# Three more split down products whose low parts VectorE makes from a bank, and four gate/up banks in place of five

## What is computed

```python
B, S, D = (2, 256, 256); I = 128; E = 32; K = 4
logits = flat @ router_w.T
scores = jnp.sqrt(jax.nn.softplus(logits))
_, idx = jax.lax.top_k(scores + expert_bias, K)
...
def _clamped_swiglu(x, wg, wu, wd):
    g = jnp.clip(x @ wg.T, -ALPHA, ALPHA)
    u = jnp.clip(x @ wu.T, -ALPHA, ALPHA)
    return jax.nn.silu(g) * u @ wd.T

def body(acc, xs):
    wg, wu, wd, p = xs
    return (acc + p[:, None] * _clamped_swiglu(flat, wg, wu, wd), None)
out, _ = jax.lax.scan(body, jnp.zeros_like(flat), (gate_w, up_w, down_w, probs.T))
out = out + _clamped_swiglu(flat, shared_gate_w, shared_up_w, shared_down_w)
x = x + out
```

## Time and profile before

| | |
|---|---|
| median of three runs | 72.20 us (72.13, 72.20, 73.02) |
| the profiled execution | 72.16 us, of which the span 70.3 us |
| granted clock of TensorE | 0.997 of full speed |
| TensorE, busy | 65.7 us (93%) |
| POOL, busy | 54.0 us (77%) |
| VectorE, ScalarE, busy | 46.9 us (67%), 46.0 us (65%) |
| read from HBM | 15.52 MB |

### The profile page before, as it was taken

The page is one execution under the profiler, slowest core; times in us unless marked ns, Lnnn a source line. Parts: engine busy times, 40 slices in busy tenths (PEclk is TensorE's granted clock), DMA queues, the critical chain, the costliest instruction groups (busy, mean ns, idle before and its releaser), DMA issues.

```text
span 70.3 us, 1581 instructions
## 1 busy us (share of the span) xinstructions
PE 65.7 (93%) x544; PEld 49.2 (70%) x546; DVE 46.9 (67%) x132; ACT 46.0 (65%) x101; POOL 54.0 (77%) x59
## 2 busy tenths in 40 slices
PE   5999998998998999999999999999999999999940
PEld 2347565787864486648787878888887888788830
DVE  0058489584779536599999907758995887697440
ACT  0604547669988665678989399999968852275220
POOL 6430005499999994999799999999999999999000
PEclk9999999999999999999999999999999999999998
DMA  0899999999999999999999997100000000000002
GB/s 0 261 282 304 343 424 390 235 332 422 429 410 408 389 403 400 403 374 347 384 415 394 396 389 274 54 6 0 0 9 0 0 0 0 0 0 0 5 0 75
DMA packets 6343, 15.75 MB, mean 224 GB/s; under 512 B 704, under 2 KB 1472, under 8 KB 6336
## 3 DMA queue, kind: packets, MB, share of 16 engines
q1 hardware_dynamic: 6048, 15.39, 59.7%
q10 hardware_dynamic: 288, 0.27, 1.1%
HBM read 15.52 MB, written 0.13 MB: 223 GB/s over the span
## 4 chain that ended last, share of the span: by engine, by line
PE 82%; DVE 7%; ACT 4%; POOL 3%; issue 1%
PE bP L581 22%; PE bY L614 7%; PE bY L603 6%; PE bE L444 6%; PE bE L581 6%; PE bXT L593 5%; PE bP L567 5%; PE bP L381 4%; PE bY L616 3%; PE bP L408 2%; DVE shifted L851 2%; POOL gu_w L347 2%; DVE row_max L849 2%; PE bXT L437 1%; ACT probs L669 1%
## 5 line engine op out<-in xcount | busy, mean ns | idle before, releaser
L347 POOL TENSOR_TENSOR gu_w<-gu_raw,gu_w 128x512 fp32r<-128x512 f32 x28 | 35.1, 1287 | 1.4 <-ACT gu_w L699 1.4
L581 PE MATMUL bP<-gu_w,xnT_parts 128*128 128x512 f32 x66 | 18.7, 418 | 0.0
L581 PEld LDWEIGHTS bP<-gu_w,xnT_parts 128*128 128x128 f32 x66 | 12.2, 189 | 3.0 <-issue 0.5
L1009 DVE SCALAR_TENSOR_TENSOR h<-gu_clip,gate,bP 128x128 f32<-128x128 f32 x26 | 7.8, 344 | 5.3 <-ACT bP L784 5.3
L955 DVE TENSOR_SCALAR gu_clip<-bP,clip_at 128x512 f32<-128x512 f32 x13 | 10.4, 806 | 1.1 <-PE bP L581 1.1
L692 ACT ACTIVATE gu_w<-gu_raw 128x1024 fp32r<-128x1024 f32 x9 | 9.4, 1048 | 1.1 <-issue 1.1
L353 POOL TENSOR_TENSOR gu_w<-dn_w,gu_w 128x512 fp32r<-128x512 f32 x8 | 10.0, 1309 | 0.0
L790 ACT ACTIVATE hT_parts<-bXT 128x256 fp32r<-128x256 f32 x11 | 4.2, 384 | 6.4 <-PE bXT L593 6.4
L784 ACT ACTIVATE bP<-gu_clip,rstd 128x256 f32<-128x256 f32 x13 | 6.2, 473 | 0.2 <-DVE gu_clip L955 0.2
L593 PE MATMUL bXT<-consts_sb,h 128*128 128x128 f32 x33 | 6.2, 271 | 0.0
L337 POOL TENSOR_TENSOR aw_sb<-aw_sb,lora_v 128x256 f32<-128x256 f32 x2 | 1.4, 727 | 6.1 <-DMA aw_sb<-attn_w_dram 6.1
(11 more groups left out here) (162 smaller groups left out, 124.3 us busy)
## 6 DMA issues: line engine op xcount, KB each, us to landing
gu_raw<-moe_w_dram SPq DMA_DIRECT2D x16, 512.0 KB, 9.7
dn_w<-moe_w_dram SPq DMA_DIRECT2D x16, 256.0 KB, 9.7
aw_sb<-attn_w_dram SPq DMA_DIRECT2D x2, 512.0 KB, 7.0
shared_sb<-shared_w_dram SPq DMA_DIRECT2D x1, 384.0 KB, 14.5
small_sb<-small_dram SPq DMA_DIRECT2D x1, 370.0 KB, 6.9
xwq_sb<-x_wq_dram SPq DMA_DIRECT2D x1, 256.0 KB, 3.5
lora_sb<-lora_dram SPq DMA_DIRECT2D x1, 256.0 KB, 4.3
ctx_sb<-ctx_kv_dram ACTq DMA_DIRECT2D x1, 192.0 KB, 3.1
```

The lines of the kernel that those rows point to most:

```text
L347: nc.gpsimd.tensor_tensor(gu_w[:, gu_slot(p), 1, cols], gu_raw[:, raw_slot(p), cols], gu_w[:, gu_slot(p), 0, cols], ALU.subtract).then_inc ...
L581: last = nc.tensor.matmul(bGU[n % 5][:, 0:GU], xnT_parts[:, a, k, :], gu_w[:, gu_slot(n - 1), w, k * GU:(k + 1) * GU], start=(k == 0 and a ...
L1009: last = nc.vector.scalar_tensor_tensor(h[:, n % 4, e], gu_clip[:, n % 4, e, 1, :], weight_e, bank[:, e * 2 * I:e * 2 * I + I], ALU.mult, ...
```

## The change

`LAST` goes from 11 to 14, so `FIRST` is 2 and units 3 to 16 have split down products. The low parts of the first three (units 3, 4, 5) are made by VectorE instead of POOL. VectorE does not read the raw weights: ScalarE first copies them into a bank (`dn_stage`), and VectorE subtracts the high part from the bank. The bank is bE, the fifth of the gate/up banks, which unit 4 is the last to use; units 6 to 16 go round over four banks, so that from unit 9 on `gate_up(n)` waits for `gate_h(n - 4)`, not `gate_h(n - 5)`. POOL makes eleven low parts as before, now those of units 6 to 16, and starts them behind pair 14 instead of 12. In ScalarE's loop `hT_unit(n)` and the new copies stand ahead of `gu_high(10 + n)`, not behind it.

```diff
-LAST = 11
-BETWEEN = 12
+LAST = 14
+STAGED = 3
+BETWEEN = 14
 FIRST = PAIRS - LAST
...
-        bGU = (bP[0][:, 0], bP[0][:, 1], bP[1][:, 0], bP[1][:, 1], bE)
+        bStage = bE
+
+        def bGU(n):
+
+            if n < 6:
+                return (bP[0][:, 0], bP[0][:, 1], bP[1][:, 0], bP[1][:, 1], bE)[n % 5]
+            return (bP[0][:, 1], bP[1][:, 0], bP[1][:, 1], bP[0][:, 0])[(n - 6) % 4]
...
                 if p >= BETWEEN:
-                    dn_low(p - BETWEEN)
-            for i in range(PAIRS - BETWEEN, LAST):
+                    dn_low(STAGED + p - BETWEEN)
+            for i in range(STAGED + PAIRS - BETWEEN, LAST):
                 dn_low(i)
...
             def gate_up(n):
 
                 if n > 5:
-                    pe.wait_ge(h_ready, n - 4)
+                    pe.wait_ge(h_ready, n - 4 if n < 9 else n - 3)
...
                     i = n - 1 - FIRST
-                    pe.wait_ge(dn_lo_ready, i + 1)
+                    if i < STAGED:
+                        pe.wait_ge(dn_lo_dve_ready, i + 1)
+                    else:
+                        pe.wait_ge(dn_lo_ready, i - STAGED + 1)
                     pe.wait_ge(hT_low_ready, i + 1)
...
+            def dn_stage(i):
+
+                if i:
+                    act.wait_ge(dn_lo_dve_ready, i)
+                else:
+                    act.wait_ge(h_ready, 5)
+                at = (FIRST + i) * 2 * D
+                nc.scalar.activation(bStage[:], dn_w[:, at:at + 2 * D], ACT.Copy).then_inc(stage_ready, 1)
+
...
             for n in range(1, PAIRS + 1):
                 if n + 2 <= PAIRS:
                     silu_unit(n + 2)
+                if 0 <= n - 2 < STAGED:
+                    dn_high(n - 2)
+                    dn_stage(n - 2)
+                hT_unit(n)
                 if EARLY + n < PAIRS:
                     gu_high(EARLY + n)
-                hT_unit(n)
-                if 0 <= n - 2 < UNITS:
-                    dn_high(n - 2)
...
+            def dn_low(i):
+
+                dve.wait_ge(stage_ready, i + 1)
+                dve.wait_ge(dn_hi_ready, i + 1)
+                nc.vector.tensor_tensor(dn_parts(i)[:, 1], bStage[:], dn_parts(i)[:, 0], ALU.subtract
+                                        ).then_inc(dn_lo_dve_ready, 1)
+
             for n in range(2, PAIRS + 1):
                 gate_h(n)
                 if n + 2 <= PAIRS:
                     clip(n + 2)
+                if 0 <= n - 4 < STAGED:
+                    dn_low(n - 4)
                 if n - 2 > FIRST:
                     hT_low(n - 2)
```

More of the change, by code:

```diff
@@ L254, in build @@
         dn_lo_ready = sem("dn_lo_ready")
+        dn_lo_dve_ready = sem("dn_lo_dve_ready")
+        stage_ready = sem("stage_ready")
         gu_hi_ready = sem("gu_hi_ready")
@@ L565, in gate_up_whole @@
             def gate_up_whole(n, k):
-                return nc.tensor.matmul(bGU[n % 5][:, 0:GU], xfT[:, k, :], gu_raw[:, raw_slot(n - 1), k * GU:(k + 1) * GU],
+                return nc.tensor.matmul(bGU(n)[:, 0:GU], xfT[:, k, :], gu_raw[:, raw_slot(n - 1), k * GU:(k + 1) * GU],
                                         start=(k == 0), stop=(k == DC - 1))
@@ L580, in gate_up @@
                         for a, w in HI_LO:
-                            last = nc.tensor.matmul(bGU[n % 5][:, 0:GU], xnT_parts[:, a, k, :],
+                            last = nc.tensor.matmul(bGU(n)[:, 0:GU], xnT_parts[:, a, k, :],
                                                     gu_w[:, gu_slot(n - 1), w, k * GU:(k + 1) * GU],
@@ L781, in silu_unit @@
                 width = 2 if n else 1
-                bank = bGU[n % 5] if n else bShared
+                bank = bGU(n) if n else bShared
                 dst = bank[:, 0:width * 2 * I].rearrange("p (e w i) -> p e w i", e=width, w=2)[:, :, 0, :]
```

## The result

The changed kernel took 75.06 us at the median of five executions (74.95 to 77.26), the kernel before 72.20 us; the ratio is 1.039, 95% interval 1.035 to 1.044. It is slower, by 2.9 us where 0.3 were forecast, and outside the forecast range (71.7 to 73.1).

What follows compares the result with a forecast made beforehand. TensorE alone was taken to bound the experts' part. The 0.46 us gain is taken and 0.8 given back at the wait before down(7): 72.16 + 0.34 = 72.5 us, range 71.7 to 73.1.

Steps and rivals of the forecast that it cites:

- the start of the sum: The kernel before's profiled time of 72.16 us, taken as the base to which the later start of down(7) was added.
- part 2: POOL's low part for down(7): without slips over at 54.00, asked for by TensorE at 54.27, slack 0.27 us.
- Part 1: Down(3), (4) and (5) become split, each shortening TensorE's path by 0.155 us: 0.46 us in all.
- Parts 3 and 4: ScalarE's queue falls 1.1 us behind by pair 13; POOL, waiting for its high parts, slips 0.93 us in sum.
- the last term of the sum: Start of down(7) moves from 54.73 to 55.00, +0.27 us, plus 0.07 for the weight load waiting with it.
- Part 5: VectorE's added subtracts and hT_low, and four banks: TensorE waits 0.05 and 0.07 us, inside the wait before down(7).
- The gain in full: Rival: ScalarE catches up, POOL slips under 0.3 us, nobody waits: 71.7 us, up to 72.2; 25%.
- VectorE slows POOL: Rival: POOL stands during VectorE's three subtracts, 0.69 us each, giving 73.9 us; 4%.
- A dear copy into the bank: Rival: `dn_stage` or the wait before it costs over 0.61 us start to start; 0.7 gives 73.0; 11%.

Runs made afterwards that it cites:

- the extra copy: Changed kernel with one more 128x512 ScalarE copy behind the first copy into the bank: 73.21 to 75.39 us, experts' part 40.92 against 40.42.
- The profile with direct subtracts: Changed kernel without the copies into the bank, VectorE subtracting from the raw weights in SBUF: 73.20 to 77.29 us, experts' part 40.90.

## Why the prediction was wrong

**The step that failed: the start of the sum.** It missed by 2.6 us (75.06 for 72.5), of which 1.9 are a term that its sum didn't have. The sum starts from 72.16, the one profiled execution, and takes the stretch before the first gate/up product as it was: a term put at nothing, without a reason. In the changed kernel TensorE's pace rose late, at 9.59 us in place of 5.10, and the first gate/up product started at 28.72 us in place of 26.84. The profile shows it for one of the five recorded executions; the times of the other four, 75.0 to 77.3, say the same. The range was built from the experts' part alone, though the kernel before has executions 2 us above its median as well; the three times that were shown (72.13 to 73.02) held none. The Trainium skill ("TensorE: Matmul & The Clock Gate", What's actually happening) says that the moment of the rise varies from run to run and puts its cost under 1% of a span; here the late rise cost 1.88 of 72.8 us, 2.6%.

How much of that was bad luck? That all five were late was a draw, but not a rare one: of the other twelve executions of the same kernel seven were late, and the median of all seventeen is 74.98. Where the rise was early, the changed kernel took 72.56, 73.08 and 73.30 us when it was run again, and 73.16 at the third time. For a forecast of 72.5 that is inside the range or up to 0.2 above it, and 1.1% above the kernel before. What misses even then is the 0.2 of part 2 and the 0.35 outside the span.

**Part 1** (0.155 us for a product). Right, as far as it can be read: two of them gave 0.2 to 0.4 where nobody was late, for a forecast of 0.31. What the step called "all the change can give" wasn't to be had with three.

**Parts 3 and 4** (the queue of ScalarE, the slip of POOL). Right to 0.05 us at each of the points above, and the extra copy confirms the chain nearly one for one (0.50 for 0.52). `dn_stage` was taken as 0.52 from start to start and is 0.52 to 0.53.

**Part 2 and the last term of the sum: mis-sized.** "TensorE asks for it at 54.73 - 0.46 = 54.27" and "the time moves by the start of down(7): 55.00 - 54.73 = +0.27". 54.73 is from the chain, which begins a piece where the piece before it ends by the model; 55.00 is from timelines, where the product begins to be issued. On the timeline down(7) began at 54.48, and its weight load at 54.46. So the move is 55.03 - 54.48 = 0.55, not 0.27, and the weight load, for which 0.07 was added, is no term of its own (both start at 56.91). The slack of POOL's unslipped piece was 0.02, not 0.27. Measured, the experts' part grew by 0.56, where the sum had 0.34: a term too small by 0.2 us, the mechanism being right.

**Part 5** (VectorE and the banks). VectorE's own times are right (0.68 for 0.69; hT_low(3) within 0.01), but the same mixture of chain and timeline made TensorE's waits too short. A split round is 2.33, on the timeline 2.52 where a plain one stands before it (50.43 to 52.95 before). The three new ones took 2.57, 2.65 and 2.38 (from 44.82, 47.39 and 50.04): 0.05, 0.32 and 0.05 lost, where 0.12 was forecast in all. TensorE reached down(7) at 56.15 + 0.13 = 56.28, or 54.40 with the 1.88 off, only 0.08 before its old time, in place of 0.34. I read the 0.32 as hT_low(4), over at 47.06 on that scale by 48.53 + 0.41 - 1.88, for which the transposes wait; the forecast had it need 47.05. The code has the transposes wait for it, and they start at 49.09, right behind its end at 48.94. The profile with direct subtracts names this wait, the one of the changed kernel names no releaser, so here it is argued, not shown. It has a consequence that the prediction didn't see: even without the wait for POOL the three products would have gained about 0.1 us and not 0.46.

**The rivals.** "The gain in full" fell: POOL slipped by what was forecast. "VectorE slows POOL" fell for the subtract from the bank (POOL kept its 1.25) and holds for one from SBUF, at 0.45 us each where the rival had 0.69. "A dear copy into the bank" fell: 0.60 us. The case on the slower side that did come, a late rise of the pace, was not among them: only 4% stood on more than 2% slower, all of it on POOL.

**Outside the span** the sum had no term either; 0.35 us there, in every execution of this kernel.

## What to carry to other kernels

Compare a release with a need only in the same view: the timeline's start of a weight load or a product against a timeline's end, never the chain's start, which here stood 0.25 us later and made a slack of 0.27 out of one of 0.02. Before explaining a difference of a whole kernel, split it at the first changed instruction, and look at what executions of one kernel do in the part that no edit touches; a range needs a term for that. When work is moved to spare engines, move only what their queues take without a late partner: two low parts by VectorE gained 0.2 to 0.4 us in the experts' part, three lost 0.56.

## What the runs showed of the hardware

- With nine warm-up products, TensorE's rise from 1.2 to 2.4 GHz fell to 3.6 to 5.7 us in most traces, to 9.5 in some and to 16.7 in one. The same program had it early in one execution and late in another. A rise at 9.6 us cost 1.9 us against one at 5.1, the one at 16.7 cost 4.1. With eleven warm-up products none of 24 executions was late.
- The record of the granted clock can begin at the rise (9.59 us), and the page then reads full for the slow stretch ahead of it. The pace of equal products (1.15 against 2.07 us for eight) shows it.
- A subtract of 128x512 on VectorE beside POOL's subtracts takes 0.68 us with one input in a bank and 1.45 to 1.78 with both in SBUF, and costs POOL some 0.45 as well.
- ScalarE's copy of 128x512 takes 0.58 to 0.60 us into a bank and 0.61 to 0.63 into SBUF, both 0.52 to 0.53 from start to start: the bank as destination is worth 0.02 us of latency and nothing in the queue.
- The changed kernel took 0.35 us more outside its span (2.12 to 2.20 against 1.74 to 1.88), in all executions; longer queues of small instructions in the kernel before did not (1.75 to 1.86).
